# Second attention of a graph block: masks ANDed and complemented two source tiles at a time, ten source tiles with a complement of their own instead of eight

## Chip, cores and metric

The kernel runs on one core of one Trainium2 chip. The metric is the device time of one execution in microseconds (us), lower is better. The engines are TensorE (PE for its matmuls, PEld for its weight loads), VectorE (DVE), ScalarE (ACT), GpSimd (POOL) and SyncE (SP, which only issues DMAs here).

## What is computed

Two attention blocks run one after the other over 2048 nodes with 512 features. The change touches only the second. Its part of the reference is:

```python
seq = (x @ W_seq).reshape(N, H, DH)                  # N=2048, H=16 heads, DH=32
score1 = jnp.einsum('nhd,d->hn', seq, a1)
score2 = jnp.einsum('nhd,d->hn', seq, a2)
scores = score1[:, :, None] + score2[:, None, :]
scores = jax.nn.leaky_relu(scores, negative_slope=ALPHA)
scores = scores + (1.0 - adj)[None, :, :] * MASK_VAL
attn = jax.nn.softmax(scores, axis=-1)
hidden = jnp.einsum('hij,jhd->ihd', attn, seq).reshape(N, D_IN)
hidden = hidden @ W_out + b_out
```

The leaky ReLU has two branches, and which of them holds for a pair (i, j) is decided by the sign of a sum of two numbers. So exp(score) is a product of a factor of i and a factor of j in either branch. The kernel needs no 2048 x 2048 softmax: per head it needs two 0/1 matrices, the edges whose sum is positive and the edges whose sum is not, each multiplied with its own scaled copy of `seq`.

## The kernel before

Stage 4 (`stage4`) is the second attention. It has a program for each engine, tied by semaphores; every engine executes its own program in the written order. Source nodes j are cut into NT = 16 tiles of 128, destination nodes i into two halves of 1024. For each of the HB = 16 heads, tile j goes through these steps:

- **Sign.** ACT (`head` of the scalar block, L1380) writes an fp8 mask of 128 x 2048 for the tile, from the row `s1b` and the tile's own scalar. DVE does this itself for the tiles 3, 8 and 13 (`vector_sign`, L1420). One of the 16 mask tiles is rewritten for the next head only after PE has used it (`mask_used`).
- **Mask.** DVE (`mask`, L1429) ANDs the tile with the adjacency `adjT`, as 128 x 512 words of 32 bits, in place.
- **Complement.** For the tiles of FAR, DVE (`far`, L1434) XORs adjacency and mask into `fars`: the edges whose sign is negative. For the other eight tiles (NEAR_TILES) there is a fixed matrix `nadjT` in the area `late`, made once per execution (L1184).
- **Product.** PE (`step`) multiplies mask tile and complement with the head's values `V`, once for each half. A tile of FAR costs 8 pairs of matmuls of 99 columns each (L1530, L1531). A near tile costs 8 pairs of 198 and 99 columns (L1533, L1534), since with the fixed matrix a correction has to be taken along with the mask. PE walks over the tiles of half 0 and, LAG = 4 tiles behind, over those of half 1. The order is (half, tile): (0,0) to (0,3), then (0,4), (1,0), (0,5), (1,1) and so on to (0,15), (1,11), and last (1,12) to (1,15).

Between these DVE does the other work of the heads: `values` and `take_off` prepare `V` of the next head, and `sum_parts` (L1445) empties the four PSUM banks of one half of the previous head, which is what lets PE start the same half of this head (`bank_free`). `scale`, `join`, `invert` and `norm` finish the previous head; they depend on one another in this order. In the program of before `far(n, j - 1)` stands behind `mask(n, j)`, so that another mask lies between a mask and its complement, and `vector_sign(n, b, j + 1)` stands in front of `mask(n, j)`.

All waits of one DVE instruction on results of another DVE instruction go through semaphores, as in `far`:

```python
dve.wait_ge(mask_ready, NT * n + j + 1)
dve.tensor_tensor(fars[:, FAR.index(j), :] ..., ALU.bitwise_xor).then_inc(far_ready, 1)
```

Of the kernel before, what the change touches and what calls it, by code (L numbers as in the profile page):

```python
# [18 lines left out]
U32 = mybir.dt.uint32  # L19
U8 = mybir.dt.uint8  # L20
F8 = mybir.dt.float8e4
# [1297 lines left out]
HALF = N // 2  # L1319
HT = HALF // P  # L1320
VECTOR_SIGN = (3, 8, 13)
FAR = (0, 3, 5, 7, 9, 11, 13, 14)
NEAR_TILES = tuple(j for j in range(NT) if j not in FAR)
NS = NT - len(VECTOR_SIGN)
LAG = 4
CZ = 2 * DZ


def stage4(nc, c, io, t, s, ps):
# [20 lines left out]
    with nc.Block() as block:  # L1350
        @block.sync
        def _(sp):
            def load(n, b):
                sp.dma_start(s1b[:, b, :], t["s1_rows"][n:n + 1, :].to_broadcast([P, N])).then_inc(s1_in[b], 16)
            sp.dma_start(t["wout"][:, :, :], io["L1_gnn_W_out"].rearrange("(t p) n -> p t n", p=P)).then_inc(t["wout_in"], 16)
            sp.dma_start(t["bout"][:, :], io["L1_gnn_b_out"].rearrange("(o d) -> o d", o=1).to_broadcast([P, D])
                         ).then_inc(t["wout_in"], 16)
            for n in range(HB - 2):
                sp.wait_ge(mask_ready, NT * (n + 1))
                load(n + 2, n % 2)  # L1360

        @block.scalar
# [25 lines left out]

        @block.vector
        def _(dve):  # L1390
            for i in range(2):
                dve.sem_inc(bank_free[i], 1)

# [23 lines left out]
            def vector_sign(n, b, j):  # L1417
                dve.wait_ge(mask_used, (NT - 1) * n + j + 1)
                dve.wait_ge(s1_in[b], 8 * (n - b) + 16)
                dve.tensor_scalar(masks[:, j, :], s1b[:, b, :], t["s2"][:, n, 1, j:j + 1], NEAR, ALU.is_gt, ALU.mult,  # L1420
                                  saturate=False).then_inc(vector_signs, 1)

            def mask(n, j):
                if j in VECTOR_SIGN:
                    dve.wait_ge(vector_signs, len(VECTOR_SIGN) * n + VECTOR_SIGN.index(j) + 1)
                else:
                    dve.wait_ge(signs, NS * n + sum(x not in VECTOR_SIGN for x in range(j)) + 1)
                own = masks[:, j, :].bitcast(U32).rearrange("p (t i) -> p t i", t=NT)
                dve.tensor_tensor(own, own, adjT[:, :, j, :].bitcast(U32), ALU.bitwise_and).then_inc(mask_ready, 1)  # L1429

            def far(n, j):

                dve.wait_ge(mask_ready, NT * n + j + 1)
                dve.tensor_tensor(fars[:, FAR.index(j), :].bitcast(U32).rearrange("p (t i) -> p t i", t=NT),  # L1434
                                  adjT[:, :, j, :].bitcast(U32),
                                  masks[:, j, :].bitcast(U32).rearrange("p (t i) -> p t i", t=NT), ALU.bitwise_xor
                                  ).then_inc(far_ready, 1)

            def sum_parts(n, half):

# [22 lines left out]
            def invert(n):  # L1463
                dve.wait_ge(joined, n + 1)
                dve.reciprocal(rz[:, :], hid[:, :, DH]).then_inc(inverse, 1)
# [4 lines left out]
                                  rz[:, :, None].to_broadcast([P, NT, DH]), ALU.mult).then_inc(normed, 1)  # L1470

            def head(n, b):
                for j in range(NT):
                    if j + 1 in VECTOR_SIGN:
                        vector_sign(n, b, j + 1)
                    mask(n, j)
                    if j - 1 in FAR:
                        far(n, j - 1)
                    if n > 0:
                        if j == 3:  # L1480
                            sum_parts(n - 1, 0)
                        if j == 5:
                            sum_parts(n - 1, 1)
                        if j == 13:
                            scale(n - 1)
                        if j == 14:
                            join(n - 1)
                        if j == 15:
                            invert(n - 1)
                            norm(n - 1)  # L1490
                    if n < HB - 1:
                        if j == 1:
                            values(n + 1)
                        if j == 9:
                            take_off(n + 1, 1 - b, 0)
                        if j == 11:
                            take_off(n + 1, 1 - b, 1)
            dve.wait_ge(t["seq_in"], 64)
            values(0)
# [12 lines left out]
        @block.tensor  # L1512
        def _(pe):
            pe.sem_inc(mask_used, NT - 1)

            def step(n, b, half, j):

                base = 4 * half
                if j == 0:
                    pe.wait_ge(bank_free[half], n + 1)  # L1520
                pe.wait_ge(mask_ready, NT * n + j + 1)
                if j in FAR:
                    pe.wait_ge(far_ready, len(FAR) * n + FAR.index(j) + 1)
                for i in range(HT):
                    cols = slice(half * HALF + i * P, half * HALF + (i + 1) * P)
                    out = ps[:, base + i // 2, 256 * (i % 2):256 * (i % 2) + 3 * CZ].rearrange("p (s c) -> p s c", s=3)
                    first = dict(start=(j == 0 and i % 2 == 0), stop=False, skip_group_check=True)
                    then = dict(start=False, stop=(j == NT - 1), skip_group_check=True)
                    if j in FAR:
                        pe.matmul(out[:, :, 0:DZ], masks[:, j, cols], V[:, b, j, :, 0:DZ], **first)  # L1530
                        last = pe.matmul(out[:, :, DZ:CZ], fars[:, FAR.index(j), cols], V[:, b, j, :, DZ:CZ], **then)  # L1531
                    else:
                        pe.matmul(out, masks[:, j, cols], V[:, b, j, :, :], **first)  # L1533
                        last = pe.matmul(out[:, :, DZ:CZ], nadjT[:, NEAR_TILES.index(j), cols], V[:, b, j, :, DZ:CZ], **then)  # L1534
                if j == NT - 1:
                    last.then_inc(psum_done[half], 1)
                if half and j < NT - 1:
                    last.then_inc(mask_used, 1)

            def head(n, b):  # L1540
                pe.wait_ge(split, n + 1)
                pe.wait_ge(packed, 2 * (n + 1))
                for j in range(NT):
                    step(n, b, 0, j)
                    if j >= LAG:
                        step(n, b, 1, j - LAG)
                for j in range(NT - LAG, NT):
                    step(n, b, 1, j)
            for n in range(HB):
                head(n, n % 2)  # L1550
# [127 lines left out]
def build(nc, io, out, kind="Internal"):  # L1678
# [6 lines left out]
    with ExitStack() as c:  # L1685
# [19 lines left out]
        t["adjT"] = area_a[:, 0:NT * N // 4].bitcast(F8).rearrange("p (t j i) -> p t j i", t=NT, j=NT)  # L1705
        t["s1b"] = area_a[:, NT * N // 4:].rearrange("p (b i) -> p b i", b=2)
        t["seq"] = area_b[:, 0:NT * D].rearrange("p (t d) -> p t d", t=NT)
        t["fars"] = area_b[:, NT * D:].bitcast(F8).rearrange("p (j i) -> p j i", i=N)
        t["masks"] = area_h[:, :].bitcast(F8).rearrange("p (j i) -> p j i", i=N)
        with ExitStack() as first:  # L1710
            f = FirstLayer(nc, first, area_a, area_b, late, keep)
# [34 lines left out]
```

## Time and profile before

| | |
|---|---|
| median of 3 runs | 1205.96 us (1204.72 to 1209.16) |
| the profiled execution's own time | 1206.59 us |
| its span in the trace | 1205.0 us |
| PE busy in the span | 1106.6 us (92%) |
| DVE busy | 950.7 us (79%) |
| ACT busy | 808.2 us (67%) |
| POOL busy | 124.8 us (10%) |

The shares are means over a program of several stages. Stage 4 lies between about 657 us and 1131 us of the span. In the timeline, a row gives the start of an instruction, its duration, and in brackets the idle time of the engine just before it with what ended it; consecutive alike instructions are put into one row with their summed time. On PE and DVE an instruction may start before the one ahead has ended, so the distance between two starts, and not a duration, is what an instruction takes up of its engine. I call that distance its step.

### The profile page before, as it was taken

What the parts mean: (1) busy time and instruction counts of PE and PEld (TensorE: products, weight loads), DVE (VectorE), ACT (ScalarE), POOL (GpSimd) and SP (SyncE); (2) the same over time, 40 slices, a digit from 0 to 9 for tenths busy, and PEclk for the clock granted to TensorE, in tenths of its full rate; (3) what the DMA queues carried; (4) which work ended last, traced back from release to release, by engine and by line L of the source; (5) the groups of instructions that cost most, each with busy time, mean ns of one, the idle gap of its engine ahead of it and who ended that gap; (6) DMA issues with size and microseconds to landing.
All of it is one profiled execution on the core that took longest, in us unless ns stands there. A gap on an engine that the chain in (4) does not pass through costs nothing. (4 is left out here: it accounts for less than half of the span.)

```text
span 1205.0 us, 24782 instructions
## 1 busy us (share of the span) xinstructions
PE 1106.6 (92%) x10565; PEld 765.8 (64%) x10565; DVE 950.7 (79%) x1320; ACT 808.2 (67%) x844; POOL 124.8 (10%) x143
## 2 busy tenths in 40 slices
PE   4799796999999999999896899999999999999897
PEld 3344343444444444444343899999999999999643
DVE  2381146999998999998753799999999999999365
ACT  1334237666667766666624999999999999996122
POOL 3678560000000000000000000000000000000011
PEclk9899897999999999999999899999999999999899
DMA  9530444222221121010342111111111111110311
GB/s 352 117 25 1 107 98 87 54 47 64 64 64 50 41 48 45 35 35 27 129 159 106 57 37 37 37 38 37 37 37 38 37 37 38 37 37 3 140 70 70
DMA packets 35213, 77.69 MB, mean 64 GB/s; under 512 B 5669, under 2 KB 10658, under 8 KB 33058
## 3 DMA queue, kind: packets, MB, share of 16 engines
q1 hardware_dynamic: 27314, 60.55, 14.2%
q0 software_dynamic: 7792, 15.58, 7.3%
q8 instruction: 84, 1.38, 0.5%
q14 instruction: 23, 0.19, 0.1%
HBM read 65.39 MB, written 23.21 MB: 74 GB/s over the span
## 5 line engine op out<-in xcount | busy, mean ns | idle before, releaser
L1380 ACT ACTIVATE area_h<-area_a,keep 128x2048 fp8e4<-128x2048 f32 x208 | 396.9, 1988 | 2.0 <-DMA area_a<-s_rows 2.0
L1533 PE MATMUL psum<-s_V,area_h 128*128 128x198 bf16 x2048 | 286.0, 248 | 0.0
L1534 PE MATMUL psum<-s_V,late 128*128 128x99 bf16 x2048 | 280.0, 208 | 0.0
L1530 PE MATMUL psum<-s_V,area_h 128*128 128x99 bf16 x2048 | 206.0, 210 | 11.7 <-DVE area_b L1434 11.0
L1531 PE MATMUL psum<-s_V,area_b 128*128 128x99 bf16 x2048 | 205.9, 209 | 0.0
L1533 PEld LDWEIGHTS psum<-s_V,area_h 128*128 128x128 fp8e4 x2048 | 199.7, 97 | 0.2
L1534 PEld LDWEIGHTS psum<-s_V,late 128*128 128x128 fp8e4 x2048 | 199.6, 97 | 0.0
L1530 PEld LDWEIGHTS psum<-s_V,area_h 128*128 128x128 fp8e4 x2048 | 189.5, 98 | 13.1 <-issue 12.0
L1531 PEld LDWEIGHTS psum<-s_V,area_b 128*128 128x128 fp8e4 x2048 | 189.6, 98 | 0.0
L1135 DVE CUSTOM_DVE_ANT_0 area_b<-psum,late 128x1500 f32<-128x1500 f32 x96 | 161.5, 1717 | 28.0 <-PE psum L634 18.6
L719 PE MATMUL psum<-area_h,s_WT 128*128 128x512 f32 x384 | 181.7, 598 | 0.0
L1429 DVE TENSOR_TENSOR area_h<-area_h,area_a 128x512 uint32<-128x512 uint32 x256 | 171.4, 685 | 11.1 <-ACT area_h L1380 6.6
L1124 DVE SCALAR_TENSOR_TENSOR s_W<-area_b,s_r,s_W 128x1500 f32<-128x1500 f32 x96 | 170.8, 1779 | 2.2
L930 ACT ACTIVATE area_b<-area_b,s_negm 128x1500 f32<-128x1500 f32 x96 | 147.7, 1539 | 19.8 <-DVE s_negm L1135 19.5
L634 PE MATMUL psum<-area_a 64*128 64x512 f32 (+1 forms) x576 | 143.3, 612 | 6.0 <-DVE s_negm L1135 5.8
L146 POOL DMA_INDIRECT rel_planes<-f_ones,f_flat x80 | 99.5, 1243 | 61.6 <-DMA rel_planes<-s_zero 24.1
L719 PEld LDWEIGHTS psum<-area_h,s_WT 128*128 128x128 f32 x384 | 66.9, 190 | 55.9 <-issue 55.4
L634 PEld LDWEIGHTS psum<-area_a 64*128 64x128 f32 x576 | 55.7, 191 | 68.1 <-issue 56.1
L425 PE MATMUL psum<-s_hT,s_wT 128*128 128x512 f32 x192 | 85.4, 604 | 6.6 <-ACT area_a L375 2.9
L1434 DVE TENSOR_TENSOR area_b<-area_a,area_h 128x512 uint32<-128x512 uint32 x128 | 87.6, 684 | 0.0
L876 ACT ACTIVATE s_WT<-psum 128x256 f32<-128x256 f32 x96 | 36.2, 377 | 53.4 <-PE psum L689 29.7
L1674 POOL DMA_DIRECT2D out<-s_x x16 | 8.7, 542 | 592.1 <-DVE s_x L1597 592.1
(168 smaller groups left out, 1200.0 us busy)
## 6 DMA issues: line engine op xcount, KB each, us to landing
area_a<-s_rows SPq DMA_DIRECT2D x16, 1024.0 KB, 4.6
rel_planes<-s_zero POOLq DMA_DIRECT2D x3, 2304.0 KB, 23.0
late<-rel_planes SPq DMA_DIRECT2D x36, 192.0 KB, 2.6
area_h<-in_x SPq DMA_DIRECT2D x4, 1024.0 KB, 21.5
keep<-in_adj POOLq DMA_DIRECT2D x16, 256.0 KB, 5.5
s_x<-in_x SPq DMA_DIRECT2D x16, 256.0 KB, 2.6
x<-s_x SPq DMA_DIRECT2D x16, 256.0 KB, 2.0
area_a<-adj_chunks SPq DMA_DIRECT2D x4, 1024.0 KB, 9.2
```

The costliest lines, as they stand in the source:

```text
L146: pool.indirect_dma_start(t["rel_planes"][plane].rearrange("i (j o) -> (i j) o", o=1), bass.IndirectOffsetOnAxis(ap=self.flat[0:EP, e:e + ...
L634: return pe.matmul(ps[:, 3 * half + ch, 0:cols.stop - cols.start], qk[rows, Q, p, r * P:(r + 1) * P], qk[rows, K, p, cols], start=True, st ...
L719: last = pe.matmul(ps[:, 7 if r < ET - 1 else 0, :], WT[m % 2][:, b, :], h[:, 2 * m + b, :], start=(m == order[0] and b == 0), stop=(m == ...
L930: act.activation(ex[:, hd, 0:NREL], ex[:, hd, 0:NREL], ACT.Exp, bias=negm[:, b, hd:hd + 1], scale=-1.0, accum_out=zs[:, b, hd:hd + 1]).the ...
L1124: dve.scalar_tensor_tensor(w, ex[:, hd, 0:NREL], r8[:, hd:hd + 1], w, ALU.mult, ALU.add).then_inc(added if hd < HA - 1 else w_ready, 1)
L1135: dve.tensor_tensor_reduce(ex[:, hd, 0:NREL], ps[:, 3 * (hd % 2):3 * (hd % 2) + 3, :].rearrange("p c j -> p (c j)")[:, 0:NREL], low[r % 2] ...
L1380: act.activation(masks[:, j, :], s1b[:, b, :], ACT.Relu, bias=t["s2"][:, n, 0, j:j + 1], scale=BIG, saturate=False).then_inc(signs, 1)
L1429: dve.tensor_tensor(own, own, adjT[:, :, j, :].bitcast(U32), ALU.bitwise_and).then_inc(mask_ready, 1)
L1530: pe.matmul(out[:, :, 0:DZ], masks[:, j, cols], V[:, b, j, :, 0:DZ], **first)
L1531: last = pe.matmul(out[:, :, DZ:CZ], fars[:, FAR.index(j), cols], V[:, b, j, :, DZ:CZ], **then)
L1533: pe.matmul(out, masks[:, j, cols], V[:, b, j, :, :], **first)
L1534: last = pe.matmul(out[:, :, DZ:CZ], nadjT[:, NEAR_TILES.index(j), cols], V[:, b, j, :, DZ:CZ], **then)
```

## The change

`mask` and `far` now take a pair m of source tiles, 2m and 2m + 1, in one instruction of 128 x 1024 words. FAR consists of whole pairs, (0, 1, 3, 4, 6), hence of the ten tiles 0 to 3, 6 to 9, 12 and 13; six near tiles are left. The fifth pair of complements lies in the space in `late` that the last two fixed matrices no longer need. The semaphores `mask_ready` and `far_ready` count pairs. `head` of the vector block is written over pairs, which changes the order. ACT's program is unchanged.

```diff
-FAR = (0, 3, 5, 7, 9, 11, 13, 14)
+FAR_PAIRS = (0, 1, 3, 4, 6)
+FAR = tuple(2 * m + i for m in FAR_PAIRS for i in range(2))
...
+PAIRS = NT // 2
...
-                sp.wait_ge(mask_ready, NT * (n + 1))
+                sp.wait_ge(mask_ready, PAIRS * (n + 1))
...
+            def words(tiles):
+                return tiles.bitcast(U32).rearrange("p j (t i) -> p j t i", t=NT)
+
+            def edges(m):
+                return adjT[:, :, 2 * m:2 * m + 2, :].bitcast(U32).rearrange("p t j i -> p j t i")
...
+            def mask(n, m):
+                for j in (2 * m, 2 * m + 1):
+                    if j in VECTOR_SIGN:
+                        dve.wait_ge(vector_signs, len(VECTOR_SIGN) * n + VECTOR_SIGN.index(j) + 1)
+                    else:
+                        dve.wait_ge(signs, NS * n + sum(x not in VECTOR_SIGN for x in range(j)) + 1)
+                own = words(masks[:, 2 * m:2 * m + 2, :])
+                dve.tensor_tensor(own, own, edges(m), ALU.bitwise_and).then_inc(mask_ready, 1)
+
+            def far(n, m):
+
+                dve.wait_ge(mask_ready, PAIRS * n + m + 1)
+                dve.tensor_tensor(words(fars[FAR_PAIRS.index(m)]), edges(m), words(masks[:, 2 * m:2 * m + 2, :]),
+                                  ALU.bitwise_xor).then_inc(far_ready, 1)
...
-                for j in range(NT):
-                    if j + 1 in VECTOR_SIGN:
-                        vector_sign(n, b, j + 1)
-                    mask(n, j)
-                    if j - 1 in FAR:
-                        far(n, j - 1)
-                    if n > 0:
-                        if j == 3:
-                            sum_parts(n - 1, 0)
-                        if j == 5:
-                            sum_parts(n - 1, 1)
-                        if j == 13:
-                            scale(n - 1)
-                        if j == 14:
-                            join(n - 1)
-                        if j == 15:
-                            invert(n - 1)
-                            norm(n - 1)
+                for m in range(PAIRS):
+                    for j in (2 * m, 2 * m + 1):
+                        if j in VECTOR_SIGN:
+                            vector_sign(n, b, j)
+                    mask(n, m)
+                    if n > 0 and m in (1, 2):
+                        sum_parts(n - 1, m - 1)
+                    if m in FAR_PAIRS:
+                        far(n, m)
+                    if n > 0 and m == PAIRS - 1:
+                        scale(n - 1)
+                        join(n - 1)
+                        invert(n - 1)
+                        norm(n - 1)
                     if n < HB - 1:
-                        if j == 1:
+                        if m == 0:
                             values(n + 1)
-                        if j == 9:
+                        if m == 4:
                             take_off(n + 1, 1 - b, 0)
-                        if j == 11:
+                        if m == 5:
                             take_off(n + 1, 1 - b, 1)
...
-                pe.wait_ge(mask_ready, NT * n + j + 1)
+                pe.wait_ge(mask_ready, PAIRS * n + j // 2 + 1)
                 if j in FAR:
-                    pe.wait_ge(far_ready, len(FAR) * n + FAR.index(j) + 1)
+                    pe.wait_ge(far_ready, len(FAR_PAIRS) * n + FAR_PAIRS.index(j // 2) + 1)
```

On DVE, at the start of a head in before (the two masks are tiles 0 and 1, the line after them is the complement of tile 0, L1400 and L1403 are `values`, L1420 is the sign of tile 3, L1445 is `sum_parts`):

```order
L1429 TENSOR_TENSOR area_h<-area_h,area_a 128x512 [waits s4_signs] x2
L1434 TENSOR_TENSOR area_b<-area_a,area_h 128x512 [waits s4_mask]
L1400 TENSOR_TENSOR s_tmp<-area_b,keep 128x32x32 [waits s4_rest,s4_packed]
L1403 TENSOR_TENSOR s_tmp<-keep 128x32
L1420 TENSOR_SCALAR area_h<-area_a,keep 128x2048 [waits s1_in1,s4_mask_used]
L1429 TENSOR_TENSOR area_h<-area_h,area_a 128x512 [waits s4_signs]
L1429 TENSOR_TENSOR area_h<-area_h,area_a 128x512 [waits s4_vector_signs]
L1445 TENSOR_REDUCE s_sums<-psum 128x528 [waits s4_joined,s4_scaled,s4_psum_done0]
L1429 TENSOR_TENSOR area_h<-area_h,area_a 128x512 [waits s4_summed,s4_signs]
L1434 TENSOR_TENSOR area_b<-area_a,area_h 128x512 [waits s4_mask]
L1429 TENSOR_TENSOR area_h<-area_h,area_a 128x512 [waits s4_signs]
L1445 TENSOR_REDUCE s_sums<-psum 128x528 [waits s4_joined,s4_scaled,s4_psum_done1]
```

The same place in the changed program (L1437 is `mask`, L1442 `far`, L1407 and L1410 `values`, L1427 `vector_sign`, L1451 `sum_parts`):

```order
L1437 TENSOR_TENSOR area_h<-area_h,area_a 128x1024 [waits s4_signs]
L1442 TENSOR_TENSOR area_b<-area_a,area_h 128x1024 [waits s4_mask]
L1407 TENSOR_TENSOR s_tmp<-area_b,keep 128x32x32 [waits s4_rest,s4_packed]
L1410 TENSOR_TENSOR s_tmp<-keep 128x32
L1427 TENSOR_SCALAR area_h<-area_a,keep 128x2048 [waits s1_in1,s4_mask_used]
L1437 TENSOR_TENSOR area_h<-area_h,area_a 128x1024 [waits s4_vector_signs,s4_signs]
L1451 TENSOR_REDUCE s_sums<-psum 128x528 [waits s4_joined,s4_scaled,s4_psum_done0]
L1442 TENSOR_TENSOR area_b<-area_a,area_h 128x1024 [waits s4_summed,s4_mask]
L1437 TENSOR_TENSOR area_h<-area_h,area_a 128x1024 [waits s4_signs]
L1451 TENSOR_REDUCE s_sums<-psum 128x528 [waits s4_joined,s4_scaled,s4_psum_done1]
L1437 TENSOR_TENSOR area_h<-area_h,area_a 128x1024 [waits s4_summed,s4_signs]
```

The complement of pair 0 now stands directly behind its mask, and the mask of pair 1 directly behind the sign of tile 3. Each waits for the instruction just ahead of it.

On DVE, at the end of a head in before (L1453 `scale`, L1461 `join`, L1465 `invert`, L1469 `norm`, between masks and complements of the tiles 12 to 15; the first row is the sign of tile 13):

```order
L1420 TENSOR_SCALAR area_h<-area_a,keep 128x2048 [waits s1_in0,s4_mask_used]
L1429 TENSOR_TENSOR area_h<-area_h,area_a 128x512 [waits s4_signs]
L1434 TENSOR_TENSOR area_b<-area_a,area_h 128x512 [waits s4_mask]
L1429 TENSOR_TENSOR area_h<-area_h,area_a 128x512 [waits s4_vector_signs]
L1453 TENSOR_TENSOR s_sums<-s_sums,keep 128x1056 [waits s4_summed]
L1429 TENSOR_TENSOR area_h<-area_h,area_a 128x512 [waits s4_signs]
L1434 TENSOR_TENSOR area_b<-area_a,area_h 128x512 [waits s4_mask]
L1461 TENSOR_TENSOR s_hid<-s_sums 128x528 [waits s4_normed,s4_scaled]
L1429 TENSOR_TENSOR area_h<-area_h,area_a 128x512 [waits s4_signs]
L1434 TENSOR_TENSOR area_b<-area_a,area_h 128x512 [waits s4_mask]
L1465 RECIPROCAL s_rz<-s_hid 128x16 [waits s4_joined]
L1469 TENSOR_TENSOR area_b<-s_hid,s_rz 128x16x32 [waits s4_inverse]
```

The same place in the changed program, which begins with the second `take_off` and the sign of tile 13 (L1459 `scale`, L1467 `join`, L1471 `invert`, L1475 `norm`):

```order
L1422 TENSOR_TENSOR s_V<-s_tmp 128x16x66 [waits s4_psum_done1,s4_rest]
L1427 TENSOR_SCALAR area_h<-area_a,keep 128x2048 [waits s1_in1,s4_mask_used]
L1437 TENSOR_TENSOR area_h<-area_h,area_a 128x1024 [waits s4_vector_signs,s4_signs]
L1442 TENSOR_TENSOR late<-area_a,area_h 128x1024 [waits s4_mask]
L1437 TENSOR_TENSOR area_h<-area_h,area_a 128x1024 [waits s4_signs]
L1459 TENSOR_TENSOR s_sums<-s_sums,keep 128x1056 [waits s4_summed]
L1467 TENSOR_TENSOR s_hid<-s_sums 128x528 [waits s4_normed,s4_scaled]
L1471 RECIPROCAL s_rz<-s_hid 128x16 [waits s4_joined]
L1475 TENSOR_TENSOR area_b<-s_hid,s_rz 128x16x32 [waits s4_inverse]
```

Sign, mask and complement of pair 6 now form one chain, and `scale`, `join`, `invert` and `norm` stand together behind the last mask, where before masks and complements lay between the first three.

On PE only the kind of the tiles changes: per head and half ten tiles of 99 and 99 columns and six of 198 and 99, where before there were eight of each. POOL sets ten signs to -1 instead of eight (L1249), and DVE makes six fixed matrices instead of eight (L1184). DMAs and their order stay.

## Rows read from the trace of the kernel before

**Rows 1.** Busy time by engine in four stretches, with PEclk the granted clock.

```profile
core 0: us, PE busy (x) PEld busy (x) DVE busy (x) ACT busy (x) POOL busy (x), PEclk, DMA share, GB/s
665.00:670.00 5.00, 4.90 (x51) 4.61 (x52) 4.76 (x7) 5.00 (x3) 0.00 (x0) 0.61 0.00 0
670.00:674.00 4.00, 2.97 (x57) 2.84 (x57) 2.54 (x4) 4.00 (x4) 0.00 (x0) 1.00 0.01 4
700.00:1090.00 390.00, 390.00 (x7006) 390.00 (x7004) 383.83 (x510) 369.93 (x210) 0.00 (x0) 1.00 0.10 37
897.90:926.41 28.51, 28.51 (x517) 28.51 (x514) 27.97 (x38) 26.67 (x15) 0.00 (x0) 1.00 0.11 39
```

**Rows 2.** Longest wait between 700 and 1100 us: total, times, longest.

```profile
ACT s_V L1369 <- PE psum L1534: 20.0, 11, 1.9
```

**Rows 3.** Timeline of DVE in a steady head, 897 to 927 us.

```profile
897.90 1.81 DVE L1445 TENSOR_REDUCE s_sums<-psum 128x528 f32<-128x1584 f32 x1 [0.23 <-PE psum L1534]
899.85 0.69 DVE L1429 TENSOR_TENSOR area_h<-area_h,area_a 128x512 uint32<-128x512 uint32 x1
900.47 0.68 DVE L1434 TENSOR_TENSOR area_b<-area_a,area_h 128x512 uint32<-128x512 uint32 x1
901.07 1.28 DVE L1420 TENSOR_SCALAR area_h<-area_a,keep 128x2048 fp8e4<-128x2048 f32 x1
902.26 1.28 DVE L1429 TENSOR_TENSOR area_h<-area_h,area_a 128x512 uint32<-128x512 uint32 x2
...
911.82 1.25 DVE L1453 TENSOR_TENSOR s_sums<-s_sums,keep 128x1056 f32<-128x1056 f32 x1
912.99 0.68 DVE L1429 TENSOR_TENSOR area_h<-area_h,area_a 128x512 uint32<-128x512 uint32 x1
...
914.19 0.70 DVE L1461 TENSOR_TENSOR s_hid<-s_sums 128x528 f32<-128x528 f32 x1
914.81 0.68 DVE L1429 TENSOR_TENSOR area_h<-area_h,area_a 128x512 uint32<-128x512 uint32 x1
...
918.71 1.22 DVE L1400 TENSOR_TENSOR s_tmp<-area_b,keep 128x1024 f32<-128x1024 f32 x1
919.84 0.21 DVE L1403 TENSOR_TENSOR s_tmp<-keep 128x32 f32<-128x32 f32 x1
...
926.41 1.81 DVE L1445 TENSOR_REDUCE s_sums<-psum 128x528 f32<-128x1584 f32 x1 [0.21 <-PE psum L1534]
```

**Rows 4.** Timeline of DVE after the last head, where each waits for the one ahead.

```profile
1126.03 1.81 DVE L1445 TENSOR_REDUCE s_sums<-psum 128x528 f32<-128x1584 f32 x1 [2.49 <-PE psum L1534]
1127.99 1.26 DVE L1453 TENSOR_TENSOR s_sums<-s_sums,keep 128x1056 f32<-128x1056 f32 x1
1129.28 0.71 DVE L1461 TENSOR_TENSOR s_hid<-s_sums 128x528 f32<-128x528 f32 x1
1130.02 0.25 DVE L1465 RECIPROCAL s_rz<-s_hid 128x16 f32<-128x16 f32 x1
1130.31 0.69 DVE L1469 TENSOR_TENSOR area_b<-s_hid,s_rz 128x512 f32<-128x512 f32 x1
```

**Rows 5.** Timeline of PE: first matmuls of a far, a near and the next near tile.

```profile
1097.31 0.21 PE L1530 MATMUL psum<-s_V,area_h 128*128 128x99 bf16 x1
...
1098.03 0.25 PE L1533 MATMUL psum<-s_V,area_h 128*128 128x198 bf16 x1
...
1099.09 0.25 PE L1533 MATMUL psum<-s_V,area_h 128*128 128x198 bf16 x1
```

**Rows 6.** Timeline of DVE: the mask of tile 1 of head 1.

```profile
691.14 0.69 DVE L1429 TENSOR_TENSOR area_h<-area_h,area_a 128x512 uint32<-128x512 uint32 x1 [1.20 <-ACT area_h L1380]
```

**Rows 7.** Timeline of DVE: the first two masks of head 15.

```profile
1088.00 1.28 DVE L1429 TENSOR_TENSOR area_h<-area_h,area_a 128x512 uint32<-128x512 uint32 x2
```

**Rows 8.** Timeline of PE: the wait in head 0.

```profile
673.60 0.21 PE L1530 MATMUL psum<-s_V,area_h 128*128 128x99 bf16 x1 [1.03 <-DVE area_b L1434]
```

**Rows 9.** Timeline of DVE: first instruction behind the fixed matrices.

```profile
623.98 0.69 DVE L1079 TENSOR_TENSOR s_x<-s_x,psum 128x512 f32<-128x512 f32 x1 [6.38 <-PE psum L719]
```

More of the change, by code:

```diff
@@ L1421, in vector_sign @@
                                   saturate=False).then_inc(vector_signs, 1)
[L1423 to L1437, printed above, removed]
+            def mask(n, m):
[10 more added lines that the diff above has]
+                                  ALU.bitwise_xor).then_inc(far_ready, 1)
             def sum_parts(n, half):
@@ L1530, in step @@
                         pe.matmul(out[:, :, 0:DZ], masks[:, j, cols], V[:, b, j, :, 0:DZ], **first)
-                        last = pe.matmul(out[:, :, DZ:CZ], fars[:, FAR.index(j), cols], V[:, b, j, :, DZ:CZ], **then)
+                        last = pe.matmul(out[:, :, DZ:CZ], fars[FAR.index(j) // 2][:, j % 2, cols], V[:, b, j, :, DZ:CZ], **then)
                     else:
@@ L1707, in build @@
         t["seq"] = area_b[:, 0:NT * D].rearrange("p (t d) -> p t d", t=NT)
-        t["fars"] = area_b[:, NT * D:].bitcast(F8).rearrange("p (j i) -> p j i", i=N)
+        fars = area_b[:, NT * D:].bitcast(F8).rearrange("p (m j i) -> p m j i", j=2, i=N)
+        spare = late[:, len(NEAR_TILES) * N // 4:8 * N // 4].bitcast(F8).rearrange("p (j i) -> p j i", i=N)
+        t["fars"] = [fars[:, m, :, :] if m < 4 else spare for m in range(len(FAR_PAIRS))]
         t["masks"] = area_h[:, :].bitcast(F8).rearrange("p (j i) -> p j i", i=N)
```

## Prediction

> **What bounds the kernel now.** I read the busy times by stretch first. From 700 to 1090 us PE is busy for all of 390.00 us at full clock, ACT for 369.93 and DVE for 383.83 [rows 1]. So PE sets the pace, and the reader is to see that DVE is just behind it. The waits say the same: ACT waits for PE once per head for 1.8 us (20.0 us in 11 times) [rows 2], so it has room. DVE waits for PE once per head, for 0.2 us, in front of the sum of half 1 [rows 3].
>
> One head lasts from one such sum to the next, 926.41 - 897.90 = 28.51 us [rows 3]. PE's steps give the same: 16 matmuls of a far tile take 1098.03 - 1097.31 = 0.72 us, of a near tile 1099.09 - 1098.03 = 1.06 [rows 5]. I use 0.73 and 1.05, which with 16 tile halves of each kind add up to 28.5.
>
> How much of the 28.51 us does DVE need for itself? It loses the 0.21 us in front of the sum, and 0.08 to 0.09 more, because behind a wait it can't overlap the end of the instruction ahead (a 512 word AND or XOR lasts 0.685 us, but the next one starts 0.60 after its start: 900.47 to 901.07 [rows 3]). So DVE's load is 28.51 - 0.30 = **28.2 us per head**, 1% below PE's. An edit that helps PE can gain 0.3 us per head before DVE binds, and an edit that costs DVE more than 0.3 us shows.
>
> **PE's part of the change.** Two tiles per head turn from near to far, in both halves: 4 x (1.05 - 0.73) = 1.3 us less. PE would need 27.2 us per head.
>
> **DVE's part: the size of the instructions.** No row shows an AND or XOR of 1024 words. The nearest is `values` with 1024 elements of 4 bytes, also with an access pattern in several dimensions: 919.84 - 918.71 = 1.13 us to the next start [rows 3]. Two of 512 take 1.20. So a pair saves only 0.07 us, since back to back instructions already overlap most of their fixed part. Bounds: no less than 1.06, pure elements with no fixed part (twice the slope of 1.13 - 0.60 = 0.53 for 512), and no more than the 1.22 that the instruction of that size lasts. With 13 such instructions in 14 heads that is 13 us less or 16 us more than what I take, the 1.13 of the row with the same size.
> - Masks: 8 x (1.20 - 1.13) = -0.56 us per head.
> - Complements: 5 x 1.13 - 8 x 0.60 = +0.85, because ten tiles are complemented and not eight.
> - Together +0.3.
>
> **DVE's part: the order.** An instruction that waits for the one directly ahead of it can't overlap its end. The trace shows the same instruction both ways. `scale` to the next start takes 912.99 - 911.82 = 1.17 us with a mask behind it, and 1129.28 - 1127.99 = 1.29 with `join` behind it, which waits for it. `join` takes 914.81 - 914.19 = 0.62 with a mask behind it and 1130.02 - 1129.28 = 0.74 with `invert` behind it [rows 3, 4]. Each such link costs **0.12 us**. The changed order makes nine new ones per head: complement behind its own mask for the pairs 0, 3, 4 and 6 (for pair 1 a sum lies between), mask behind its own sign for the pairs 1, 4 and 6, `join` behind `scale`, and `invert` behind `join`. In before none of the nine was there; `norm` behind `invert` was and stays. 9 x 0.12 = +1.1 us. Nothing hides this, as what is queued behind is the rest of DVE's own list, and PE waits for it. Bounds of a link: 0 (if a longer instruction covers it) and 0.18 (half as much again, for the masks that wait on two semaphores); I take the 0.12 that two different instructions show.
>
> The Trainium skill, "VectorE: DVE Perf Modes", section "The DRAIN you can't avoid", says that every DVE instruction waits until the pipe of the one ahead is empty and that chaining with semaphores costs nothing extra. By that rule the nine links would be free; the rows above speak against it. The result that it would give is the first rival below.
>
> **Sum per head.** DVE: 28.2 + 0.3 + 1.1 = **29.6 us**. PE: 27.2. ACT: 26.67 busy [rows 1], unchanged. DVE becomes the bound and PE waits 2.4 us per head, in pieces.
>
> **Does DVE itself ever wait then?** I count from the start D of a head on DVE, with steps 1.13 for pairs, 1.20 for signs (901.07 to 902.26), 1.95 for sums (897.90 to 899.85), 1.25 for `values` and 0.12 per link. The first sum ends at D + 8.0 and lets PE start half 0; the second begins at D + 10.3. Complement 4 is there at D + 18.5, complement 6 at D + 25.7, the last mask at D + 26.8. PE takes the tiles 8 to 15 of half 0 with their partners in 20 steps, ten of each kind: 17.8 us, which end at D + 36.3, that is 6.7 us into the next head, ahead of the second sum at 10.3. So DVE doesn't wait for PE. ACT finishes tile 15 about 11.5 us after that end, at 18.2 into the head, ahead of the last mask at 25.7. So DVE runs without a stop and its load counts in full.
>
> **The first and the last head.** In head 0 and at the start of head 1 DVE waits for ACT: the mask of tile 1 of head 1 starts at 691.14 us behind such a wait [rows 6]. A mask of tiles 0 and 1 needs the same two signs, so head 1 starts there after the change too. Its 14 successors: head 15 starts at 691.1 + 14 x 29.6 = 1105.5. Before it started at 1088.00 [rows 7], and the last sum, which marks the end of PE's work, came 38.0 us later, at 1126.03 [rows 4]. In head 15 `values` is gone, so complement 4 is there at 17.2, and 17.8 us of PE end at 35.0: 1140.5. Stage 4 ends **14.5 us later**. The last stage and the sums ahead of it stay. Two fixed matrices fewer and two more signs to set lie in front of a 6.38 us wait of DVE for PE [rows 9]: nothing.
>
> The profiled execution took 1206.59 us, 0.6 above the median of the runs. So I predict 1206.6 + 14.5 = 1221.1 for its like and **1220.5 us** for the median.
>
> **Rivals.**
> - *The links are free.* Then DVE needs 28.5 us, as much as PE did. Head 15 starts at 691.1 + 14 x 28.5 = 1090.1, five links less make its rest 34.4, the end is 1124.5: 1204.5 us, no change. For it: the links have to be covered by something that the two instructions of the trace don't have. Against: both show 0.12. It also covers partly hidden links. 12%.
> - *Faster: the long AND and XOR run at a better rate for each word.* The sign instruction takes only 1.20 us for 2048 elements (901.07 to 902.26 [rows 3]), so DVE has forms at twice the rate. If the pairs with their regular pattern got some of it, the place to see it is their step. It decides from 1.01 us down, where DVE needs 13 x 0.12 = 1.6 less, 28.0 per head, and at 0.95 DVE needs 27.3 like PE: 14 x 1.2 = 17 less than before, 1189 us. Against it: the sign reads one tensor, `values` reads two like AND and XOR, and takes 1.13 for 1024. 6%.
> - *PE's clock falls as well.* PE now waits several times per head. After a wait of some 10 us it was granted 0.61 in 665 to 670, that is mostly 1.2 GHz; in 670 to 674, with 1.03 us of waiting in it [rows 8], 1.00 [rows 1]. None of the new waits is longer than about 1.5 us. If the mean fell to 0.9, PE would need 30.2 per head, 0.6 more than DVE: 1229 us. 5%.
> - *As forecast*: 77%, with 1216 to 1226 as its own range, from a pair step of 1.10 to 1.15 (13 instructions, 14 heads: -5 to +4 us) and links of 0.10 to 0.14 (2.5 us either way).
>
> **How the numbers follow.** A measurement of this kernel can tell about 0.5% from no change, 6 us. The forecast and the clock's case are slower by more: 0.82. The links that are free or half covered give 0.12 within, the fast case 0.06. The range reaches from the rival without change, 1205, to 1226; it leaves out the fast case, the clock's and what lies beyond the own range of the likeliest.
>
> **What would show it.** In the changed trace, PE is no longer at 390 of 390 us but near 92% busy between 700 and 1090. DVE has 29.6 us between sums of the same half with no idle time in front of them. AND and XOR of a pair last 1.22 us, and a complement starts 1.25 and not 1.13 behind its mask. ACT waits for PE as before and a little longer, and the clock stays at 1.00. I am wrong if linked pairs follow at 1.13, if PE is still gapless, or if DVE waits for PE in front of the sums.

## The result and the profile after

Six timed executions of the changed kernel have a median of 1226.2 us (1222.38 to 1227.73), beside 1205.89 for the kernel before (1204.0 to 1209.16). The ratio is 1.0159 (95% interval 1.0142 to 1.0176): it is slower, by less than 2% but clear of no change, and by 19 us in the middle of the interval, where I had forecast 14.5. The median stands at the very end of my range, which reached to 1226. The profiled execution took 1222.50 us, with a span of 1220.9 us: each is 15.9 us more than before.

The busy times of stage 4 come first, as in [rows 1]:

```profile
core 0: us, PE busy (x) PEld busy (x) DVE busy (x) ACT busy (x) POOL busy (x), PEclk, DMA share, GB/s
700.00:1090.00 390.00, 365.66 (x6692) 357.48 (x6690) 378.72 (x341) 351.72 (x199) 0.00 (x0) 1.00 0.10 37
```

PE is busy for 365.66 of the 390 us, where it was busy for all of them before. DVE's busy time is even less than before, 378.72 us where it was 383.83. A reader who looks at shares alone would think that DVE got room. The waits between 700 and 1100 us (engine, line, waited for, us in total, times, longest) say otherwise:

```profile
ACT s_V L1371 <- DVE s_tmp L1422: 41.4, 13, 3.2
PEld psum L1532 <- issue: 30.4, 39, 1.4
PE psum L1532 <- issue: 15.9, 13, 1.2
PE psum L1532 <- DVE area_b L1442: 8.7, 14, 0.6
DVE area_h L1437 <- DVE s_sums L1451: 3.0, 14, 0.2
```

PE waits in front of far tiles (L1532 is the first matmul of one). 14 waits of up to 0.6 us are for a complement. For 13 others of up to 1.2 us the view names nothing ("issue"); that they are for the bank which DVE's sum has to empty is read from the times further down. DVE has no wait for PE left, and the 0.2 us of L1437 stand behind its own sum. Otherwise DVE's list runs without a stop. ACT, which waited for PE before [rows 2], now waits for DVE's first `take_off` (L1422). What DVE lost is overlap, and no view of waits shows that. The timeline of DVE shows it:

```profile
870.81 1.28 DVE L1427 TENSOR_SCALAR area_h<-area_a,keep 128x2048 fp8e4<-128x2048 f32 x1
872.20 1.23 DVE L1437 TENSOR_TENSOR area_h<-area_h,area_a 128x1024 uint32<-128x1024 uint32 x1
873.34 1.80 DVE L1451 TENSOR_REDUCE s_sums<-psum 128x528 f32<-128x1584 f32 x1
...
877.57 1.80 DVE L1451 TENSOR_REDUCE s_sums<-psum 128x528 f32<-128x1584 f32 x1
879.58 1.23 DVE L1437 TENSOR_TENSOR area_h<-area_h,area_a 128x1024 uint32<-128x1024 uint32 x1 [0.21 <-DVE s_sums L1451]
880.84 1.22 DVE L1442 TENSOR_TENSOR area_b<-area_a,area_h 128x1024 uint32<-128x1024 uint32 x1
881.98 1.28 DVE L1427 TENSOR_SCALAR area_h<-area_a,keep 128x2048 fp8e4<-128x2048 f32 x1
883.29 1.23 DVE L1437 TENSOR_TENSOR area_h<-area_h,area_a 128x1024 uint32<-128x1024 uint32 x1
884.55 1.22 DVE L1442 TENSOR_TENSOR area_b<-area_a,area_h 128x1024 uint32<-128x1024 uint32 x1
...
889.17 1.28 DVE L1427 TENSOR_SCALAR area_h<-area_a,keep 128x2048 fp8e4<-128x2048 f32 x1
890.56 1.23 DVE L1437 TENSOR_TENSOR area_h<-area_h,area_a 128x1024 uint32<-128x1024 uint32 x1
...
894.10 1.25 DVE L1459 TENSOR_TENSOR s_sums<-s_sums,keep 128x1056 f32<-128x1056 f32 x1
895.38 0.71 DVE L1467 TENSOR_TENSOR s_hid<-s_sums 128x528 f32<-128x528 f32 x1
896.12 0.25 DVE L1471 RECIPROCAL s_rz<-s_hid 128x16 f32<-128x16 f32 x1
...
897.02 1.22 DVE L1437 TENSOR_TENSOR area_h<-area_h,area_a 128x1024 uint32<-128x1024 uint32 x1
898.27 1.22 DVE L1442 TENSOR_TENSOR area_b<-area_a,area_h 128x1024 uint32<-128x1024 uint32 x1
...
903.19 1.80 DVE L1451 TENSOR_REDUCE s_sums<-psum 128x528 f32<-128x1584 f32 x1
...
926.88 1.22 DVE L1437 TENSOR_TENSOR area_h<-area_h,area_a 128x1024 uint32<-128x1024 uint32 x1
```

One head lasts from 897.02 to 926.88, **29.86 us**, where I had 29.6. A complement behind its own mask starts 1.26 us later (879.58 to 880.84), and what follows the complement and waits for nothing 1.14 (880.84 to 881.98). Their durations are 1.23 and 1.22. `scale`, `join` and `invert` follow one another at 1.28 and 0.74, where [rows 4] have 1.29 and 0.74. The waits of PE in one head:

```profile
905.26 0.21 PE L1532 MATMUL psum<-s_V,area_h 128*128 128x99 bf16 x1 [1.22 <-issue]
915.78 0.21 PE L1532 MATMUL psum<-s_V,area_h 128*128 128x99 bf16 x1 [0.62 <-DVE area_b L1442]
```

The first is the start of half 0, for which the first sum must be done: it starts at 903.19 and lasts 1.80, the next instruction of DVE would start at 903.19 + 1.95 = 905.14, and PE starts at 905.26. The second is tile 8, whose complement the forecast had as the point from which PE's last 20 steps count. Last the two ends of stage 4 on DVE, which answer to [rows 4, 6, 7] (the first row is `values` of head 0, the last the sum behind the end of PE):

```profile
655.51 1.23 DVE L1407 TENSOR_TENSOR s_tmp<-area_b,keep 128x1024 f32<-128x1024 f32 x1 [0.50 <-PEq L521]
...
688.02 1.23 DVE L1437 TENSOR_TENSOR area_h<-area_h,area_a 128x1024 uint32<-128x1024 uint32 x1 [2.49 <-ACT area_h L1382]
...
1106.01 1.22 DVE L1437 TENSOR_TENSOR area_h<-area_h,area_a 128x1024 uint32<-128x1024 uint32 x1
...
1141.55 1.81 DVE L1451 TENSOR_REDUCE s_sums<-psum 128x528 f32<-128x1584 f32 x1 [2.80 <-PE psum L1536]
```

**A measure of its own for stage 4.** From the first `values` to the last sum it takes 1141.55 - 655.51 = 486.0 us, and before it took 1126.03 - 657.71 = 468.3. This is +17.7, while its end moved by 15.5. The difference of 2.2 us lies ahead of stage 4, in stages whose code the change hardly touches. In the eleven traces of this study that first `values` starts anywhere between 654.9 and 661.4 us. I give stage 4's own length for every run below.

**What the trace of before says beyond [rows 3].** In the first heads DVE isn't yet held back by PE. Two sums of half 0 there, with no wait in front:

```profile
696.01 1.80 DVE L1445 TENSOR_REDUCE s_sums<-psum 128x528 f32<-128x1584 f32 x1
...
724.22 1.80 DVE L1445 TENSOR_REDUCE s_sums<-psum 128x528 f32<-128x1584 f32 x1
```

The distance is 28.21 us, and it stays at 28.21 to 28.24 for six heads before it grows to the 28.51 of PE. So the 28.2 us of DVE, which the forecast worked out, can be read directly. It also means that 28.51 holds for the later heads of before and not for all of them.

### The profile page after: what moved, and what is told of

Same layout as the page of the kernel before. It is cut to its first block and busy times, and to the rows that moved or that the text cites. A ratio compares the mean times of both kernels' runs of the same rounds, so it can differ in the third digit from the quotient of the medians.

```text
span 1220.9 us, 24793 instructions
## 1 busy us (share of the span) xinstructions
PE 1095.0 (90%) x10560; PEld 748.6 (61%) x10565; DVE 966.2 (79%) x1142; ACT 808.4 (66%) x844; POOL 124.3 (10%) x145
## 5 line engine op out<-in xcount | busy, mean ns | idle before, releaser
L1532 PE MATMUL psum<-s_V,area_h 128*128 128x99 bf16 x2560 | 256.0, 210 | 38.3 <-DVE area_b L1442 21.4
L1532 PEld LDWEIGHTS psum<-s_V,area_h 128*128 128x128 fp8e4 x2560 | 236.2, 98 | 48.5 <-issue 45.1
L1535 PE MATMUL psum<-s_V,area_h 128*128 128x198 bf16 x1536 | 214.8, 248 | 0.0
L1536 PE MATMUL psum<-s_V,late 128*128 128x99 bf16 x1536 | 210.2, 208 | 0.0
L1533 PE MATMUL psum<-s_V,area_b 128*128 128x99 bf16 x2048 | 209.3, 210 | 0.0
L1437 DVE TENSOR_TENSOR area_h<-area_h,area_a 128x1024 uint32<-128x1024 uint32 x128 | 156.4, 1222 | 12.5 <-ACT area_h L1382 5.3
L1536 PEld LDWEIGHTS psum<-s_V,late 128*128 128x128 fp8e4 x1536 | 149.5, 97 | 0.0
L1442 DVE TENSOR_TENSOR area_b<-area_a,area_h 128x1024 uint32<-128x1024 uint32 x64 | 78.4, 1225 | 3.9
```

The costliest lines, as they stand in the source:

```text
L1437: dve.tensor_tensor(own, own, edges(m), ALU.bitwise_and).then_inc(mask_ready, 1)
L1533: last = pe.matmul(out[:, :, DZ:CZ], fars[FAR.index(j) // 2][:, j % 2, cols], V[:, b, j, :, DZ:CZ], **then)
```

## The experiments

Each was timed beside the kernel before. `Stage 4` is the length defined above, and `head` the distance between two sums of the same half in the middle of it (for before, in the later heads).

| kernel | median us | ratio to before (95%) | stage 4 us | head us |
|---|---|---|---|---|
| before | 1205.89 | | 468.3 | 28.51 |
| the change | 1226.20 | 1.0159 (1.0142 to 1.0176) | 486.0 | 29.85 |
| 1 the change again | 1222.50 | 1.0133 (1.0108 to 1.0158) | 486.3 | 29.85 |
| 2 links taken away, order A | 1222.91 | 1.0130 (1.0100 to 1.0159) | 485.3 | 29.53 |
| 3 single tiles, eight links | 1216.63 | 1.0070 (1.0045 to 1.0094) | 476.3 | 29.20 |
| 4 order A, nine far tiles | 1235.60 | 1.0233 (1.0204 to 1.0263) | 494.6 | 30.15 |
| 5 links taken away, order B | 1207.11 | 1.0000 (0.9984 to 1.0016) | 466.9 | 28.39 |
| 6 order B, nine far tiles | 1202.42 | 0.9968 (0.9952 to 0.9985) | 462.1 | 27.87 |
| 7 the change, two waits swapped | 1221.96 | 1.0140 (1.0104 to 1.0175) | 484.2 | 29.71 |
| 8 single tiles, ten far | 1220.22 | 1.0112 (1.0076 to 1.0148) | 478.9 | 29.41 |
| 9 order A, complement 4 earlier | 1211.79 | 1.0054 (1.0034 to 1.0074) | 473.1 | 28.75 |

**1. The change again,** unaltered.

> The changed kernel once more, unaltered, beside the other three. Its six timed executions lay in two groups, two at 1222.4 us and four at 1225.7 to 1227.7 with a mean granted clock of 0.971 to 0.974 in place of 0.976; the trace that I have is one of the first group. If DVE's load alone makes the time, a trace of the second group has the same 29.86 us per head in stage 4 and its extra 4 us lie elsewhere. If PE's clock falls now and then because PE waits in stage 4, the granted clock of 700 to 1090 us is below 1.00 there.

All four executions lay at 1221.7 to 1223.1 us, with mean granted clocks of 0.976 to 0.978. The trace is like the first one to 0.2 us. So the group at 1225.7 to 1227.7 did not come back, and no trace of it exists. Swapped waits (7) showed two such groups again, 1219.2 and 1219.4 at 0.977 and 1224.5 and 1224.9 at 0.972, and the kernel before reaches from 1201.9 at 0.980 to 1211.2 at 0.970. A kernel's executions thus spread by several us, before and after the change alike, and the longer ones mostly have the lower mean granted clock. PE's granted clock from 700 to 1090 us was 1.00 in every trace of the study, so I suppose that the spread comes from outside that stretch, but this was not shown.

**3. One part alone: links without pairs.** The kernel before, with a complement directly behind its mask:

```diff
-                    if j - 1 in FAR:
-                        far(n, j - 1)
+                    if j in FAR:
+                        far(n, j)
```

> The kernel before with one edit: each of the eight complements directly behind its own mask. Single tiles, FAR and everything else as before. Theory (a link costs 0.12 us and DVE has 0.3 us to spare): DVE needs 28.2 + 8 x 0.12 = 29.2 us per head and becomes the bound, time 1212 to 1216, PE waits some 0.7 us per head. Rival (links are free or covered): 1206, PE gapless.

The median is 1216.63, 0.6 above the forecast and 9.4 above the 1207.2 of before beside it. Two sums of half 0:

```profile
902.84 1.80 DVE L1445 TENSOR_REDUCE s_sums<-psum 128x528 f32<-128x1584 f32 x1
...
932.04 1.80 DVE L1445 TENSOR_REDUCE s_sums<-psum 128x528 f32<-128x1584 f32 x1
```

The distance is 29.20 us, as counted, and no sum between 700 and 1090 us has a wait in front. PE waited 7.6 us in 12 times, again with nothing named, in front of a far tile. Nothing but the order of the same instructions changed. Eight links make DVE's 28.21 us 0.99 longer, 0.12 for each, and all but 0.3 of it shows. This run shows both the price of a link between mask and complement and how little DVE had to spare.

**8. The other part alone: ten far tiles without pairs.** `FAR = (0, 1, 2, 3, 6, 7, 8, 9, 12, 13)` in the kernel before, the two further complements in the free part of `late`.

> The kernel before with one edit: the ten far tiles of the change, still one tile at a time and in the old order without new links. Theory (DVE's load is the bound once it passes PE's): 28.2 + 2 x 0.60 = 29.4 us per head, time 1216 to 1220; the saving of 1.1 us per head on PE is lost whole. Rival (PE's saving counts, since the two engines only have to keep up on the mean): 1200 or less.

It came out at 1220.22 and 29.41 us per head. The busy times of 700 to 1090 us:

```profile
700.00:1090.00 390.00, 368.80 (x6788) 362.21 (x6789) 385.45 (x517) 358.38 (x203) 0.00 (x0) 1.00 0.10 37
```

The 29.41 us are DVE's 28.21 and two complements of 0.60. PE had 1.3 us per head less to do and stood idle for 1.6 (21.2 of 390 us). The choice of far tiles shifts work from PE to DVE, and DVE had no room for it.

**2 and 4. All links taken away, order A.** This order puts a complement one mask behind its own, a sign one mask ahead, and `scale` one mask earlier:

```diff
+                    for j in (2 * m + 2, 2 * m + 3):
...
                     mask(n, m)
+                    if n > 0 and m == PAIRS - 1:
+                        join(n - 1)
+                    if m - 1 in FAR_PAIRS:
+                        far(n, m - 1)
...
+                    if n > 0 and m == PAIRS - 2:
+                        scale(n - 1)
...
```

> The changed kernel with another order on DVE: a complement one mask behind its own mask, a sign one mask ahead of its own mask, join and invert apart. All nine new links are gone, the pairs and the ten complements stay. Theory (links of 0.12 us make the most of the loss, 1.3 us per head with the longer ones): DVE needs 28.5 us per head, PE 27.2, time 1205 to 1208, as before the change. Rival (the loss is the size of the work on DVE, two complements more): no change against the changed kernel, 1220 or more.

> The relaxed order with nine complements: tile 13 is near again, and the fifth complement instruction takes one tile. Theory: DVE needs 28.0 us per head, PE 27.9, both below the 28.5 of before; time 1197 to 1200, faster than both kernels. Rival (what DVE saves is lost because PE then waits for masks or DVE for PE, with both engines full): 1205.

Both missed. Order A lasts 29.53 us per head, nine far tiles with it 30.15. Taken alone this spoke for the rival, that the amount of work is the loss. The traces spoke against it, because DVE waited in front of both sums, 0.45 and 0.23 us in order A and 1.31 and 0.54 with nine tiles. An engine that waits once per head can't be the one that alone sets the pace. Timeline of DVE in order A, from the second sum (908.96) to complement 4 (919.09) and to the next second sum:

```profile
908.96 1.81 DVE L1451 TENSOR_REDUCE s_sums<-psum 128x528 f32<-128x1584 f32 x1 [0.23 <-PE psum L1538]
910.98 1.28 DVE L1427 TENSOR_SCALAR area_h<-area_a,keep 128x2048 fp8e4<-128x2048 f32 x1 [0.22 <-DVE s_sums L1451]
912.19 2.35 DVE L1437 TENSOR_TENSOR area_h<-area_h,area_a 128x1024 uint32<-128x1024 uint32 x2
914.46 1.22 DVE L1442 TENSOR_TENSOR area_b<-area_a,area_h 128x1024 uint32<-128x1024 uint32 x1
915.59 1.25 DVE L1422 TENSOR_TENSOR s_tmp<-s_tmp 128x1056 f32<-128x1056 f32 x1
916.76 1.28 DVE L1427 TENSOR_SCALAR area_h<-area_a,keep 128x2048 fp8e4<-128x2048 f32 x1
917.96 1.22 DVE L1437 TENSOR_TENSOR area_h<-area_h,area_a 128x1024 uint32<-128x1024 uint32 x1
919.09 1.22 DVE L1442 TENSOR_TENSOR area_b<-area_a,area_h 128x1024 uint32<-128x1024 uint32 x1
...
938.49 1.81 DVE L1451 TENSOR_REDUCE s_sums<-psum 128x528 f32<-128x1584 f32 x1 [0.23 <-PE psum L1538]
```

And PE's waits in the same head (L1534 is the first matmul of a far tile):

```profile
915.82 0.21 PE L1534 MATMUL psum<-s_V,area_h 128*128 128x99 bf16 x1 [0.38 <-DVE area_b L1442]
920.45 0.21 PE L1534 MATMUL psum<-s_V,area_h 128*128 128x99 bf16 x1 [1.54 <-DVE area_b L1442]
```

These are the complements of the pairs 3 and 4. In order A a take-off, the sign of tile 13 and mask 5 had come in front of complement 4. From the end of a head on PE the work goes through the second sum and DVE's list to complement 4, which is there 10.1 + 1.2 = 11.3 us later, and then through the 18 us that PE has left from tile 8 on: 29.4 us, and the head takes 29.53. Neither engine is full. With nine far tiles PE has more to do behind the same wait: tile 13 is near in both halves, 2 x 0.32 us more, so the 29.53 us become 30.2, and 30.15 were measured.

**9. The same order with one instruction moved.** If that loop is the cause, complement 4 alone, moved behind complement 3, has to open it:

```diff
-                    if m - 1 in FAR_PAIRS:
+                    if m - 1 in FAR_PAIRS and m != 5:
                         far(n, m - 1)
+                    if m == 4:
+                        far(n, 4)
```

> The first relaxed order with one instruction moved: complement 4 directly behind complement 3, ahead of the take-off, the sign of tile 13 and mask 5. No link comes or goes. Theory (there the loop was: end of a head on PE, second sum, DVE's list up to complement 4, then 18 us of PE): the wait of 1.54 us for complement 4 goes, complement 6 may be waited for by up to 1 us, and DVE's load of 28.5 us sets the pace; 28.5 to 28.6 us per head in place of 29.53, time 1206 to 1210 in place of 1222.9. Rival (the place of complement 4 has nothing to do with it): 29.5 us per head.

Two sums of half 0, and between them the sum of half 1 with the complement ahead of it:

```profile
896.69 1.80 DVE L1451 TENSOR_REDUCE s_sums<-psum 128x528 f32<-128x1584 f32 x1
...
899.84 1.22 DVE L1442 TENSOR_TENSOR area_b<-area_a,area_h 128x1024 uint32<-128x1024 uint32 x1
901.06 1.81 DVE L1451 TENSOR_REDUCE s_sums<-psum 128x528 f32<-128x1584 f32 x1
...
925.44 1.81 DVE L1451 TENSOR_REDUCE s_sums<-psum 128x528 f32<-128x1584 f32 x1
```

The distance is 28.75 us, the waits of 0.45 and 0.23 us in front of the sums are gone from the middle of the stage, and the time falls from 1222.9 to 1211.79 (as a ratio to before, from 1.0130 to 1.0054). That is 2 us above what I expected. PE's wait for complement 4 is gone, one of 0.37 for complement 3 stays, and one of 0.76 for complement 6 appeared. Of the 0.25 us above the 28.5 that I had counted for DVE, 0.14 are longer starts behind the two sums (2.01 and 2.03 us where 1.95 was counted). Another 0.08 stand in front of the sum of half 1: it starts 1.22 us behind a complement, where 1.14 is the usual distance. PE's last matmul of that head starts at 900.82 and lasts 0.21, so the sum starts as PE ends. So a loop is still just closed, now through complement 6, less than 0.1 us above DVE's load; this was read from the trace and not tested. The place of complement 4 was the cause of most of the loss in 2. For 4 it follows from the sum above and not from a run of its own.

**5 and 6. Links taken away with PE served first, order B.** The list of a head: mask 0, join, complement 0, invert, sign 3, values, norm, mask 1, sign 8, sum, complement 1, mask 2, sum, masks 3 and 4, complements 3 and 4, take-off, mask 5, sign 13, take-off, masks 6 and 7, complement 6, scale, with join, invert and norm one head later than before.

```diff
+                mask(n, 3)
+                mask(n, 4)
+                far(n, 3)
+                far(n, 4)
+                if n < HB - 1:
+                    take_off(n + 1, 1 - b, 0)
```

> The relaxed order failed to help although its links were gone: its trace shows PE waiting 0.38 us for complement 3 and 1.54 us for complement 4 in each head, because a take-off and the sign of tile 13 had come in front of complement 4, and DVE then waiting for PE in front of the sums. This order takes the links away without that: the sign of tile 8 ahead of the first sum, masks 3 and 4, then complements 3 and 4, directly behind the second sum; masks 6 and 7 and then complement 6; scale at the end of the head, and join, invert and norm between masks and complements of the next one. Ten complements, pairs as in the change. Theory (links, with PE served in time): DVE needs 28.4 us per head and sets the pace, time 1203 to 1208. Rival A (what DVE has to do for ten complements is the loss): 1220. Rival B (a loop through both engines that no order of DVE's list avoids): PE waits for complements again, 1215 or more.

> The same order with nine complements: tile 13 is near, the fifth complement instruction takes one tile of 512 words. Theory: DVE needs 27.9 us per head, PE 27.9 to 28.1, in place of 28.5 before; time 1197 to 1202. Rival B (the loop through both engines): 1210 or more.

Ten far tiles in order B, two sums of half 0:

```profile
898.38 1.80 DVE L1451 TENSOR_REDUCE s_sums<-psum 128x528 f32<-128x1584 f32 x1
...
926.77 1.80 DVE L1451 TENSOR_REDUCE s_sums<-psum 128x528 f32<-128x1584 f32 x1
```

The head takes 28.39 us and the kernel 1207.11, ratio 1.0000 (0.9984 to 1.0016). This kernel has the pairs and the ten complements of the change and differs only in DVE's order. So with another order the whole loss of the change is gone. DVE still sets the pace: no sum waits in the middle of the stage, while PE waits once per head for complement 3, up to 1.0 us, so that what the change saves on PE stays unused. The head is 1.46 us shorter than with the change. The nine links are 1.22 of that by the starts above; another 0.12 is the old link of `norm` behind `invert`, which this order takes away as well (0.29 us between the starts with the change, and 0.17 from `invert` to the next instruction here). With nine far tiles a head takes 27.87 us, the median is 1202.42, and the ratio 0.9968 (0.9952 to 0.9985) is clear of 1 but small: 4 us. The expectation of 1197 to 1202 was missed by a little. Its busy times of 700 to 1090 us:

```profile
700.00:1090.00 390.00, 389.61 (x7144) 389.49 (x7142) 384.59 (x364) 374.07 (x212) 0.00 (x0) 1.00 0.10 37
```

PE is at 389.61 us, and no sum of DVE waits before the last head: both engines are as good as full. This kernel is faster than both the kernel before and the change.

**7. Two waits swapped.** In the trace of the change the mask followed its sign after 1.39 us in the pairs 1 and 6, and in pair 4 after 1.31 (870.81 to 872.20, 889.17 to 890.56 and 881.98 to 883.29 above). In pair 4 the wait for DVE's own sign is the first of the two, in the others the second.

```diff
-                for j in (2 * m, 2 * m + 1):
+                for j in sorted((2 * m, 2 * m + 1), key=lambda x: x not in VECTOR_SIGN):
```

> The changed kernel with one edit: for the pairs 1 and 6 the wait for the sign that DVE makes stands ahead of the wait for ACT's sign, as it does for pair 4 already. In the trace of the change the mask follows its sign after 1.39 us in the pairs 1 and 6 and after 1.31 in pair 4, where a sign with something else behind it takes 1.19. Theory (the place of the wait that blocks makes the difference): 1.31 in all three, 0.16 us less per head, 29.70, time 2 us less than the change. Rival (the tile or the place in the list makes it): still 1.39.

The pairs 1 and 6 and two sums of half 0:

```profile
869.69 1.28 DVE L1427 TENSOR_SCALAR area_h<-area_a,keep 128x2048 fp8e4<-128x2048 f32 x1
871.01 1.23 DVE L1437 TENSOR_TENSOR area_h<-area_h,area_a 128x1024 uint32<-128x1024 uint32 x1
872.15 1.80 DVE L1451 TENSOR_REDUCE s_sums<-psum 128x528 f32<-128x1584 f32 x1
...
887.98 1.28 DVE L1427 TENSOR_SCALAR area_h<-area_a,keep 128x2048 fp8e4<-128x2048 f32 x1
889.29 1.23 DVE L1437 TENSOR_TENSOR area_h<-area_h,area_a 128x1024 uint32<-128x1024 uint32 x1
...
901.86 1.80 DVE L1451 TENSOR_REDUCE s_sums<-psum 128x528 f32<-128x1584 f32 x1
```

The mask now follows after 1.32 and 1.31 us, and the head takes 29.71. Stage 4 is 1.8 us shorter than in the first trace of the change and 2.0 shorter than in the second, where 2 were expected. The timed medians spread too far to show this.

## Why the prediction was right, and where it was off

- **The bound before.** PE full, DVE 0.3 us behind it per head: right. Experiments 3 and 8 add 0.96 and 1.2 us to DVE's list in two different ways and lengthen a head by 0.69 and 0.90, each as 28.2 plus the addition says. The first heads of before show the 28.21 directly.
- **The size of the pairs.** A pair step of 1.14 (1.13 taken) and a duration of 1.22 to 1.23: right. Merging two instructions of 512 words saves 0.06 to 0.07 us of DVE's time, though the durations alone (2 x 0.685 against 1.22) would suggest 0.15.
- **The order.** 0.12 us for a link: right for seven of the nine, by the starts in the trace of the change, and shown for mask and complement by 3. For the masks of the pairs 1 and 6 it was 0.20, above the 0.18 that I had put as its upper end. This term was mis-sized by 0.16 us per head. Another 0.06 came from the mask behind the second sum, at 2.01 (877.57 to 879.58) where 1.95 was taken. Together they are 0.22 of the 0.26 by which the head was longer than forecast; the pair steps of 1.14 are in the rest.
- **DVE never waits, PE waits in pieces.** Right: 1.22 us at the start of half 0 and 0.62 at tile 8. Their sum of 1.8 is less than the 2.4 of the forecast, and PE is 94% busy (365.66 of 390) where I had named 92%. In part this is how the profile counts: the last matmul ahead of a wait is busy for 0.21 us, while a matmul in the stream takes up 0.05. The clock stayed at 1.00.
- **What ACT waits for.** Wrong: I had said that ACT would wait for PE as before. It waits for DVE's `take_off`, 41.4 us in 13 times up to 3.2, where it waited 20.0 us for PE before. Nothing hangs on it, since the time is DVE's.
- **The ends.** Head 1 began 32.5 us after the first `values` where 33.4 was taken, head 15 to the last sum took 35.5 where 35.0 was. The sum in stage 4 is then 14.5 - 0.9 + 3.6 (14 x 0.26) + 0.5 = 17.7, the measured value.
- **The time.** So the sum was 3.2 us short in stage 4, mostly by the order's term. The remaining 1.5 us to the 19.2 us of the ratio are not in the two traces, which are 15.9 apart; I put them down to the spread of the executions, whose cause is open. The first six executions have their median at the end of the range, and the four repeated ones well inside it (1222.5). Which of the two a set shows is up to that spread and not to the forecast.
- **The first rival,** free links, falls with 3: eight links cost 0.99 us per head. The Trainium skill, "VectorE: DVE Perf Modes", section "The DRAIN you can't avoid", says of eight copies that a semaphore behind each costs nothing extra. That doesn't carry over to these instructions, where a wait for the one just ahead costs 0.12 us. The same section adds that a next instruction which isn't held starts earlier, which the prediction left out; the traces agree, with 0.60 us between starts for a duration of 0.685 [rows 3].

What I had not thought of belongs to the experiments and not to the prediction: my first order without links forgot that PE needs complement 4 early. The prediction had the positions at which PE needs each complement, and I did not count them again for the new order.

## What to carry to other kernels

Where instructions overlap, as on DVE here, take the load of the engine as the sum of the distances between starts, not of durations or busy times. It depends on the order: the same list cost 28.2 or 29.2 us per head by where its dependent pairs stood. Merging instructions pays only the part that wasn't overlapped already, so check what the merge does to the order before counting its gain. When two engines are both nearly full, as here with 1% between them, put first what the other one waits for, and then keep dependent instructions apart. Order A did only the second and cost 29.53 us per head, close to the 29.85 of the links.

## What was unexpected of the hardware

- Of two semaphore waits ahead of one DVE instruction, the place of the one that blocks matters: blocked at the second, the instruction starts 1.39 us after the start of a sign of 1.28, and blocked at the first 1.31. Experiment 7 shows this for the pairs 1 and 6.
- A pair mask directly behind a sum starts 2.01 us after it and a complement 1.95 (875.29 behind the sum at 873.34 in the trace of the change), though each waits for the sum ahead of it. The pair mask has three waits in the program and the complement two. The mask of one tile in before has two and takes 1.95 [rows 3], and the sign behind a sum in order A has three and takes 2.02. So it may be the number of waits, but no run tests this, and the cause is open.
